# A layer of attention and gated FFN on eight cores: half of the first x loads and the wu loads move from SyncE's DMA queue to ScalarE's, the second-half wd loads the other way

## What is computed

```python
xn = layernorm(x)                                   # no scale or shift
q, k, v = xn @ Wq.T + bq, xn @ Wk.T + bk, xn @ Wv.T + bv
q, k = rope(split_heads(q)), rope(split_heads(k))
scores = where(causal, q @ k^T / sqrt(64), -inf)
s = merge_heads(softmax(scores) @ v) @ Wo.T + bo
h = silu(xn @ (w_gate/127).T) * (xn @ (w_up/127).T) # int weights, 3072 hidden
g = silu(h @ (w_down/127).T)
out = x + s * g
```

## Time and profile before

| | us |
|---|---|
| runs of the kernel before | 4193.38 and 4427.04, median 4310.21 |
| the profiled execution | 4188.53 |
| its span on the slowest core (core 4) | 4187.0 |
| spans of all cores | 4161.4 to 4187.0 |
| stage 0, LayerNorm and transpose | 0 to about 213 |
| stage 1, attention | about 213 to 2597 |
| stage 2, FFN | about 2597 to 4187 |

### The profile page before, as it was taken

The page is one execution under the profiler, slowest core; times in us unless marked ns, Lnnn a source line. Parts: engine busy times, 40 slices in busy tenths (PEclk is TensorE's granted clock), DMA queues, the critical chain, the costliest instruction groups (busy, mean ns, idle before and its releaser), DMA issues.

```text
span 4187.0 us, 38065 instructions; the slowest of 8 cores (4161.4 to 4187.0 us)
## 1 busy us (share of the span) xinstructions
PE 2812.2 (67%) x12576; PEld 1132.5 (27%) x12800; DVE 769.9 (18%) x1600; ACT 1495.7 (36%) x1475; POOL 82.4 (2%) x117
## 2 busy tenths in 40 slices
PE   1176656676656676656766664788786868787787
PEld 1132211231212231211411211333242423333333
DVE  3321131121221211210210310111111111111111
ACT  2226616536436356356266265211111111111111
POOL 0000010000000000000100000000000000000000
PEclk9997868888868878878978787899999999999999
DMA  4230040030030020110300002334343424343333
GB/s 116 76 48 0 0 53 1 10 39 0 13 41 1 21 28 0 27 27 0 71 0 1 21 0 48 98 101 142 98 140 97 141 97 136 107 129 111 121 121 106
DMA packets 221229, 250.06 MB, mean 60 GB/s; under 512 B 101584, under 2 KB 150736, under 8 KB 220400
## 3 DMA queue, kind: packets, MB, share of 16 engines
q1 hardware_dynamic: 81408, 142.65, 11.0%
q0 software_dynamic: 84336, 29.45, 6.3%
q10 hardware_dynamic: 55296, 75.52, 6.0%
HBM read 241.25 MB, written 35.65 MB: 66 GB/s over the span
## 4 chain that ended last, share of the span: by engine, by line
PE 45%; ACT 25%; DMA 11%; issue 8%; DVE 8%; SPq 3%; ACTq 1%; DVEq 0%; POOL 0%; POOLq 0%
ACT SCR L584 12%; PE S L564 9%; PE S L843 8%; ACT SCR L598 8%; PE S L855 8%; DMA SCR<-wsc 5%; DMA SCR<-SCR 3%; PE C L440 3%; PE C L639 3%; PE S L824 3%; SPq L99 3%; PE S L796 2%; PE S L913 2%; DMA SCR<-x 1%; ACT rct L486 1%
## 5 line engine op out<-in xcount | busy, mean ns | idle before, releaser
L564 PE MATMUL S<-SCR 64*128 64x512 bf16 (+3 forms) x2304 | 451.7, 440 | 581.2 <-ACT SCR L584 263.8
L584 ACT ACTIVATE SCR<-S 128x3072 bf16<-128x3072 f32 x224 | 611.7, 2731 | 308.8 <-PE S L564 308.8
L639 PE MATMUL C<-SCR 128*128 128x512 bf16 (+3 forms) x2208 | 621.8, 420 | 126.4 <-DVE ctxT L502 61.8
L598 ACT ACTIVATE SCR<-S 128x1536 bf16<-128x1536 f32 (+3 forms) x320 | 381.4, 1195 | 444.1 <-PE S L564 434.2
L843 PE MATMUL S<-xnT,SCR 128*128 128x512 bf16 x1510 | 377.7, 393 | 4.3 <-issue 1.5
L865 ACT ACTIVATE xnT<-S 128x512 bf16<-128x512 f32 x192 | 114.7, 597 | 726.5 <-PE S L843 723.5
L564 PEld LDWEIGHTS S<-SCR 64*128 64x128 bf16 x2304 | 130.9, 102 | 896.7 <-issue 861.2
L392 PE MATMUL S<-xnT,SCR 128*128 128x512 bf16 x1007 | 281.4, 441 | 133.9 <-DVE SCR L400 130.9
L855 PE MATMUL S<-xnT,SCR 128*128 128x512 bf16 x1496 | 360.6, 381 | 2.1
L639 PEld LDWEIGHTS C<-SCR 128*128 128x128 bf16 x2304 | 209.3, 107 | 518.9 <-issue 406.2
L613 DVE TENSOR_TENSOR SCR<-SCR,tri_s 128x128 bf16<-128x128 bf16 x512 | 80.9, 220 | 1232.7 <-ACT SCR L598 1232.5
(11 more groups left out here) (77 smaller groups left out, 1622.2 us busy)
## 6 DMA issues: line engine op xcount, KB each, us to landing
SCR<-wsc ACTq DMA_DIRECT2D x192, 256.0 KB, 2.7
SCR<-wsc SPq DMA_DIRECT2D x192, 256.0 KB, 2.8
SCR<-wsc SPq DMA_DIRECT2D x192, 128.0 KB, 2.1
SCR<-wsc ACTq DMA_DIRECT2D x192, 128.0 KB, 2.1
ctxT<-x SPq DMA_DIRECT2D x32, 512.0 KB, 3.5
SCR<-SCR SPq DMA_DIRECT2D x256, 64.0 KB, 2.0
SCR<-x SPq DMA_DIRECT2D x32, 512.0 KB, 4.5
out<-SCR SPq DMA_DIRECT2D x32, 512.0 KB, 2.8
```

The source lines that it names most:

```text
L564: S_=Sreg, i_=it, kl=klo: te.matmul(S_[0:128, o:o + w_], Kg[kl:kl + 64, j * 128:(j + 1) * 128], Qg[kl:kl + 64, i_ * 512 + r_: i_ * 512 + r ...
L584: etok = E("act", lambda sc, P_=Pb: sc.activation(P_[:, 0:3072], S6.ap()[:, 0:3072], AF.Exp, scale=0.125), after=(specs[0][9], specs[1][9] ...
L598: etok = E("act", lambda sc, w_=wexp, h_=h2, P_=Pb: sc.activation(P_[:, h_ * 1536: h_ * 1536 + w_], S6.ap()[:, h_ * 1536: h_ * 1536 + w_], ...
L639: sp=(is_diag and kk == len(grp) - 1): te.matmul(C_.ap()[0:128, r_:r_ + w_], Vt[:, j * 130 + v_: j * 130 + v_ + 128], P_[:, h_ * 1536 + o: ...
```

## The change

Four DMAs get another issuing engine. Nothing else changes: no size, no buffer, no wait, and no place in the text.

1. In stage 0 the x loads of odd row tiles (16 of 32, 512 KB each) are issued by ScalarE; the even ones stay on SyncE.
2. In `loadA` (chunks 0 and 1 of every iteration) wu moves from SyncE to ScalarE.
3. In loop A `wu(hc + 2)` moves from SyncE to ScalarE. With 2 this is all 192 loads of wu.
4. In `loadB` (all 192 loads of wdB) the load moves from ScalarE to SyncE.

```diff
-            xt = DMA("sp", xq_sl[sl], xsl[sl][:, :], xin[rt * 128:(rt + 1) * 128, :],
-                     after=b_xsl[sl].wr())
+            xt = DMA("sp" if rt % 2 == 0 else "act", xq_sl[sl], xsl[sl][:, :],
+                     xin[rt * 128:(rt + 1) * 128, :], after=b_xsl[sl].wr())
...
             t = DMA("act", wgs_s[sl], wg_sl[sl], wsc[0, hc], after=b_wg[sl].wr() + tuple(fence))
             b_wg[sl].setw(t)
-            t = DMA("sp", wus_s[sl], wu_sl[sl], wsc[1, hc], after=b_wu[sl].wr() + tuple(fence))
+            t = DMA("act", wus_s[sl], wu_sl[sl], wsc[1, hc], after=b_wu[sl].wr() + tuple(fence))
...
         def loadB(hc):
             sl = hc % 2
-            t = DMA("act", wdBs_s[sl], wdB_sl[sl], wsc[2, hc][:, 512:1024],
+            t = DMA("sp", wdBs_s[sl], wdB_sl[sl], wsc[2, hc][:, 512:1024],
                     after=b_wdB[sl].wr() + tuple(fence))
...
-                    t = DMA("sp", wus_s[slw], wu_sl[slw], wsc[1, hc + 2],
+                    t = DMA("act", wus_s[slw], wu_sl[slw], wsc[1, hc + 2],
                             after=b_wu[slw].wr() + tuple(fence))
```

## The result

The changed kernel is slower by half a per cent. The median of all its runs is 4220.88 us against 4193.68 us for the kernel before; the ratio of comparable runs is 1.0055 with a 95% interval of 1.0042 to 1.0069, about 23 us. The forecast was +4 us. In about a third of the executions of either kernel some cores show a lower granted TensorE clock and the time is 1.5 to 6% longer; the ratio leaves these out, and where a profiled execution has such cores (0 to 3 in that of the changed kernel, 4 to 7 in that of the run wu back on SyncE) the other four are read. Rows of the changed kernel and of the experiments are of core 6, those of the kernel before of core 4, unless said otherwise.

A forecast was written before the change was run, and what follows sets the result against it. TensorE was read as the engine everything feeds, waiting for weights only in loop B, with stage 0 a chain of tiles. 7.4 - 3.7 + 0 + 2.8 - 2.5 = +4.0 us on 4188.53 gave 4193 us; range 4166 to 4320.

The forecast's parts named there:

- the one on stage 0: Rival: stage 0 loses its prefetch in full, +27 to +31 us, about 4214 us in all; chance 12 in 100.
- Edit 1, the mechanism: Stage 0: odd x loads go out 0.08 us after normalization starts; each odd tile stalls 0.46 us, +7.4 us in all.
- my own sign, a wait at L319 above 1 us: Stage 0 statistics: expected x waits of about 0.46 us, 16 times; one above 1 us would show the prediction wrong.
- Edits 2 and 3, the wait on the up matmuls costs nothing: Loop A: ScalarE's new wait before issuing wu fits within 2.4 us of slack, 192 times; cost 0.
- hc == 12, -3.7 us: Loop A at hc == 12: without wu ahead, x goes out 0.43 us sooner; 7 x 0.53 = -3.7 us.
- the backlog's effect: At hc == 12: wu no longer right in front of x, taken as 0.1 us from nothing to 0.7 us.
- Edit 4, the trip is as long from SyncE: Loop B: wdB's round trip, 88 in all, is unchanged from SyncE; 0, bounds -4 and +4 us.
- The head of loop B, +2.8 us with an upper bound of +8.4: Loop B's start: 1 MB of wg and wu runs beside the first two wdB loads; 0.4 us for each of seven iterations.
- my half share: Head of loop B: DMA engines take turns between queues, so a wdB load gets half and needs up to 0.6 us more.
- The end of loop B, -2.5 us: Before the first SiLU L940: without loadB(1) ahead, the gap shrinks from 0.94 to 0.59 us; 7 x 0.35 = -2.5 us.
- The wide upper end of 4320: Whole kernel: range extended to 4320 us because one of two runs of the same program was 5.6% longer.

The follow-up runs named there:

- wu back on SyncE: The kernel of three repairs with all wu loads issued by SyncE again, at the same places; ratio to the kernel before 0.9837.
- the change again: The full change, unaltered, profiled again as a reference for other runs; one comparable execution, 4219.49 us, no ratio on record.
- edit 4 alone: The kernel before with only the wdB loads of loadB moved from ScalarE to SyncE; ratio to before 1.0001.
- three repairs: The full change plus odd x loads one tile sooner, next iteration's wg and wu at hc == 22 and 23, x loads at hc == 5; ratio to before 0.9858.

## Why the prediction was right or wrong

That it would be within 2% and slower by a little was right, but as a size +4 us is not +23. The measured ratio lies inside the forecast's own bounds of -10 to +38. No rival describes it: the one on stage 0 comes near in time (4214), but it wanted +27 to +31 from stage 0, which gave +10.9. By the steps of the working:

- *Edit 1, the mechanism:* right. The DMA goes out 0.01 us after the start of the normalization (I had taken 0.08 from a SiLU), lands 3.6 us later, and the stall is 0.47 us in the mean where 0.46 was worked out. *Its size:* +10.9 and not +7.4, because I took 16 equal tiles. The load of tile 1 takes 7.05 us: a stall of 4.0 us once. By my own sign, a wait at L319 above 1 us, the working was wrong there. The 5.0 us at the upper end of the earlier trace rows was a hint that landing times at the beginning are others.
- *Edits 2 and 3, the wait on the up matmuls costs nothing:* right in this kernel (loops A 925.6 and 923.0). It holds only while something else at hc == 12 is later still. With x in time, the same wait costs 16 us.
- *hc == 12, -3.7 us:* wrong, though the table's -2.6 looks close. x is issued 0.4 us sooner, but it lands that much later: 4.7 us in the median after, 4.3 before. TensorE's idle time before the first transposes is 6.8 us in the mean before and 6.7 after on cores 4 to 7, where I had taken off 0.53. I had set the backlog's effect at -0.1; it ate the gain. Where the 2.6 us come from isn't shown, and the change again doesn't have them.
- *Edit 4, the trip is as long from SyncE:* right, and shown by the last loop B, which is 42.7 and 42.8 us.
- *The head of loop B, +2.8 us with an upper bound of +8.4:* the step that failed; it measured +17.6. Two things were wrong in it. I wrote that wg and wu "stand today on ScalarE behind the wdB loads", but wu of loadA stood on SyncE and had been issued ahead of loop B, at 2762 and 2766, and so had wdA, which I didn't follow at all. So 768 KB came newly into loop B. And the term was built from a wdB load that gets half of the engines. Measured, the first wait rises from 0.7 to 2.9 us in the mean, by 2.2 us and not by 0.4; seven times 2.2 is 15 of the 17.6. The Trainium skill (DMA: Bandwidth & Descriptors, "Queues, rings and completion order") says beside the taking of turns that the increment of a DMA's semaphore lands only after every earlier write of that engine, across its queues. The rows fit that better than my half share: wdB, issued 1.3 us after the first of the four, is complete after more than 4 us and not 2.7. No run here separates the two. What is shown: moving wg and wu ahead of loop B takes all of the loss away, 25 us against the change, with wdB still on SyncE. Holding `loadA` back and spreading it take none of it away, but they exchange waits for slower matmuls, and edit 4 alone loses about half as much with as many bytes. The price of one load isn't known from these runs.
- *The end of loop B, -2.5 us:* the gap went to 0.58 as worked out, but the tails gained 6.0. The rest goes with the clock, which I had left out. In the first iteration 3.09 us of idleness stand before the projection's next 47 matmuls in the kernel before, and they took 12.21 us; in the row above it is 2.73 us, and 48 took 10.52. Over the 28 projections of cores 4 to 7 the short time is seen 6 times before and 16 times after; ten more at 1.7 us are 4 us for each core, and with 7 x 0.36 = 2.5 us that covers the 6.0. The length of the idleness alone doesn't decide it: one core of the kernel before has the short time four times, all after 3.09 or 3.10 us.

The sum of what was measured, 10.9 - 2.6 + 17.6 + 0.1 - 6.0 = +20.0, leaves 3 us of 23 that I can't place; attention differs by more than that between cores.

The wide upper end of 4320 came from the spread of two runs and not from a mechanism. The forecast's own range of 4178 to 4226 would have been enough. That is partly luck: the upper bound owes 31 us to stage 0, where 10.9 was measured, while the term that failed measured twice its own upper bound of 8.4.

## What to carry to other kernels

A DMA belongs in the list of an engine that has nothing in front of it to wait for. When it is moved to a computing engine, write down when it was issued before and when it will be, for each place in the text that issues it, prologues of the next iteration included: here the moved loads of the steady loop cost nothing, and those at its seams cost 17 us. Follow also the loads that weren't moved but stand behind a moved one. Where a loop is bound by a chain of small loads, look at all that moves while it runs: on each chip here the kernel with more beside the chain had the longer loop, at a price that depends on the order, and the loads belong before the loop where their buffers are free. Compare waits and busy time apart before two equal sums are taken for one cause. And ask of the largest wait of the profile first whether its load could simply be issued sooner: one such edit was worth 67 us, three times all that the four edits of this change moved.

## What the runs showed of the hardware

- A DMA behind an activation in ScalarE's list was issued 0.01 us after the start of the normalization and 0.07 to 0.08 us after that of a SiLU. But an activation behind a DMA waits for the issue: 0.36 us of the gap before L940 (0.94 against 0.58).
- 128 KB that landed in 2.1 us in the median of the kernel before took over 4 us at the head of loop B, when 1 MB was issued on the other queue from 1.3 us before it to the same moment; 512 KB took 3.5 us in the median of stage 0, and 7.05 us beside the last of GpSimd's weight loads.
- After short idleness TensorE's matmuls went on at either clock: before the projection, 2.73 us were followed by 48 matmuls in 10.52 us and 3.09 us by 47 in 12.21, but both times occur after both. At hc == 12 with three repairs, 1.03 us of idleness with a second one of 1.59 right after it was followed by eight matmuls in 3.29 us in place of 1.89.
